# Filter matrices from sixteen skewed copies of the taps, and v kept unflipped in the first phase

## The reference, cut to what matters

```
q_in = silu(causal_dwconv(h @ Wq, wq_conv))     # 4 taps; k_in and v_in alike
q, k = l2norm(q), l2norm(k)
inv  = -(k*beta @ k.T) * strict_lower           # per chunk of 32 tokens
for i in range(1, 32): inv[i] += inv[i] @ inv   # row by row
local_long  = causal_dwconv(v_in, fir_long)     # 64 taps, a filter of its own per channel
local_short = causal_dwconv(v_in, fir_short)    # 5 taps
```

## Time and profile before

| what | value |
|---|---|
| median of 3 runs | 1322.98 us (1320.78 to 1327.27) |
| the profiled execution's own time | 1323.56 us |
| its span, first to last instruction | 1321.8 us |
| busy, share of the span | PE 85%, DVE 72%, ACT 68%, POOL 49% |
| mean granted TensorE clock | 0.895 |
| first phase, second phase | 0 to 240.7 us, 240.7 to 319.8 us |

### The profile page before, as it was taken

The page is one execution under the profiler, slowest core; times in us unless marked ns, Lnnn a source line. Parts: engine busy times, 40 slices in busy tenths (PEclk is TensorE's granted clock), DMA queues, the critical chain, the costliest instruction groups (busy, mean ns, idle before and its releaser), DMA issues. The chain is left out here.

```text
span 1321.8 us, 28637 instructions
## 1 busy us (share of the span) xinstructions
PE 1119.9 (85%) x9251; PEld 820.2 (62%) x9251; DVE 958.0 (72%) x2132; ACT 898.0 (68%) x1743; POOL 653.0 (49%) x2200
## 2 busy tenths in 40 slices
PE   5998988783678799999999999999999888885756
PEld 4776766683566566766776776676677655443225
DVE  5999998698355657777877877777787566633985
ACT  5999998221344558787878878877887665453867
POOL 4777775563225544465465466547546543111007
PEclk9999998555557869999999999999999988897989
DMA  2443433893412434343433434343442342203106
GB/s 80 159 176 144 177 136 144 185 234 107 137 57 85 110 80 127 95 124 109 133 110 106 146 105 138 106 129 105 111 144 82 96 127 57 65 33 140 44 1 223
DMA packets 141779, 154.17 MB, mean 117 GB/s; under 512 B 48040, under 2 KB 106560, under 8 KB 141632
## 3 DMA queue, kind: packets, MB, share of 16 engines
q1 hardware_dynamic: 141632, 152.35, 38.4%
HBM read 93.32 MB, written 58.72 MB: 115 GB/s over the span
## 5 line engine op out<-in xcount | busy, mean ns | idle before, releaser
L2120 DVE TENSOR_REDUCE x_maxima<-x_psA 128x2 f32<-128x512 f32 x248 | 170.3, 687 | 96.2 <-PE x_psA L1448 93.7
L1704 ACT ACTIVATE x_PT<-x_psB 128x512 f32<-128x512 f32 x240 | 143.0, 596 | 56.5 <-PE x_psB L1472 52.1
L1711 ACT ACTIVATE x_psA<-x_mask_q 128x512 f32<-128x512 bf16 x239 | 142.4, 596 | 51.8 <-DVE x_maxima L2120 48.7
L297 DVE SCALAR_TENSOR_TENSOR a_conv<-a_ps_proj,taps,a_conv 128x253 f32<-128x253 f32 (+2 forms) x288 | 115.0, 471 | 8.4 <-ACT a_conv L364 8.4
L1448 PE MATMUL x_psA<-x_Ks,x_Qs 96*128 96x256 bf16 x496 | 99.5, 283 | 15.2 <-ACT x_psA L1711 14.7
L1469 PE MATMUL x_psB<-x_mask_k,x_ident_bf 128*128 128x512 bf16 x240 | 94.3, 393 | 13.0 <-ACT x_PT L1704 10.8
L533 PE MATMUL a_ps_proj<-a_hT,wqkv 128*128 128x256 f32 x384 | 93.2, 392 | 7.1 <-DVE a_conv L297 4.2
L1472 PE MATMUL x_psB<-x_Qs,x_Ks 98*128 98x256 bf16 x480 | 94.1, 277 | 0.0
L533 PEld LDWEIGHTS a_ps_proj<-a_hT,wqkv 128*128 128x128 f32 x384 | 71.5, 194 | 19.4 <-issue 6.6
L1864 POOL TENSOR_SCALAR x_parts_q<-x_rest 128x512 bf16<-128x512 f32 x16 | 23.9, 1494 | 116.3 <-DVE x_rest L2096 116.3
L1486 PE MATMUL x_psO<-x_PT,x_V 128*32 128x256 f32 x1024 | 72.0, 401 | 1.0 <-ACT x_PT L1704 1.0
(11 more groups left out here) (390 smaller groups left out, 3352.8 us busy)
## 6 DMA issues: line engine op xcount, KB each, us to landing
scratch_keypack<-a_keypack SPq DMA_DIRECT2D x16, 768.0 KB, 3.3
c_keypack<-scratch_keypack SPq DMA_DIRECT2D x16, 768.0 KB, 4.7
x_Ks<-scratch_k_parts SPq DMA_DIRECT2D x192, 64.0 KB, 2.2
b_matrix<-in_long_padded SPq DMA_DIRECT2D x16, 512.0 KB, 7.4
scratch_k_parts<-x_parts_k SPq DMA_DIRECT2D x32, 192.0 KB, 2.4
scratch_q_parts<-x_parts_q SPq DMA_DIRECT2D x32, 192.0 KB, 2.3
x_Qs<-scratch_q_parts SPq DMA_DIRECT2D x32, 192.0 KB, 3.0
a_x_in<-in_x SPq DMA_DIRECT2D x16, 256.0 KB, 2.7
```

Source lines behind the costliest of these rows:

```text
L297: nc.vector.scalar_tensor_tensor(acc, ps_proj[PROJ_BANK[p]][:, c, 0:L - j], taps[:, p, c, TAPS - 1 - j:TAPS - j], acc, ALU.mult, ALU.add). ...
L1704: nc.scalar.activation(PT[:, k % (2 * GROUP)], bank_B(b, k)[0], ACT.Exp, scale=XD ** -0.5).then_inc(pexp_ready, 1)
L1711: nc.scalar.activation(psA[:].rearrange("p t q -> p (t q)"), mask_q[:, k % 2].rearrange("p s k -> p (s k)"), ACT.Copy).then_inc(mask_writt ...
L2120: nc.vector.tensor_reduce(maxima[:, t, 2 * pair:2 * pair + 2], bank_A(b, k)[0], AX.X, ALU.max).then_inc(maxed, 1)
```

## The change

The filter matrices get their reversal from memory instead of from PE. The taps are copied once, DRAM to DRAM, into 16 copies one behind the other for each channel. A transfer to 16 neighbouring partitions then reads with a step of `FIR_COLS - 1` from one copy to the next, which is one tap back per partition, the direction that unflipped v needs. The matrices of all 256 channels stay in SBUF (`keep["matrix"]`, 64 KB per partition) and are loaded in the first phase, one transfer per turn (`taps`, stage 1: 16 partitions by 128 channels by 64 taps). All flips and their evictions go; `vtok` writes straight into `v_windows`, `st_v` stores from there, and two small DMAs (`win`) make the second, shifted window. The second phase has no matrix loads: groups of 8 channels in each of two halves, one matmul of 64 columns per channel, eight PSUM banks. To make room, `diag` and all but one quarter of `M` live in `X32`, so the transposes of DVE (first and last) wait for one another, and POOL waits for all four; other small buffers share space.

```diff
-           ... (2, "turn_h"), (2, "hTc"), (5, "flipA"), (4, "ktok"), (5, "st_p"), (4, "st_k"),
+           ... (2, "turn_h"), (2, "hTc"), (4, "ktok"), (5, "st_p"), (4, "st_k"), (1, "taps"),
-           (4, "stok"), (1, "xn"), (4, "flipB"), (2, "gbias"), (4, "ks"), (4, "ksT"), (3, "tok1"), (4, "fB"), (3, "sq1"),
+           (4, "stok"), (1, "xn"), (2, "gbias"), (4, "ks"), (4, "ksT"), (3, "tok1"), (3, "sq1"),
...
+                elif op == "taps":
+                    row, half = b // FC, b % FC
+                    sp.wait_ge(taps_copied, 16)
+                    taps_of = bass.AP(dram["taps_copies"].tensor, half * P * COPIES * FIR_COLS + P - 1 - COPIES * row,
+                                      [[FIR_COLS - 1, COPIES], [COPIES * FIR_COLS, P], [1, HB]])
+                    sp.dma_start(keep["matrix"][COPIES * row:COPIES * row + COPIES, half * P:half * P + P], taps_of).then_inc(taps_placed, 16)
+                elif op == "win":
+                    sp.wait_ge(v_tok_ready, b + 1)
+                    sp.dma_start(keep["v_windows"][HB:P, 0, :, b], keep["v_windows"][0:HB, 1, :, b]).then_inc(window_set, 16)
+                    sp.dma_start(keep["v_windows"][0:HB, 0, 1, b], keep["v_windows"][HB:P, 1, 0, b]).then_inc(window_set, 16)
...
-            sp.dma_start(flip[:], dram["flip"]).then_inc(w_loaded, 16)
-            sp.dma_start(half_flip[:], dram["half_flip"]).then_inc(w_loaded, 16)
+            sp.dma_start(dram["taps_copies"], bass.AP(dram["long_padded"].tensor, 0, [[FIR_COLS, D], [0, COPIES], [1, FIR_COLS]])).then_inc(taps_copied, 16)
...
-                    nc.scalar.activation(v_tok[:], ps_tok[2][:], ACT.Copy).then_inc(v_tok_ready, 1)
-                elif op == "fA":
...
+                    nc.scalar.activation(keep["v_windows"][:, 1, :, b], ps_tok[2][:], ACT.Copy).then_inc(v_tok_ready, 1)
...
-CG = 16
-GROUPS = D // CG
-DEPTH = 4
+CG = 8
+GROUPS = P // CG
+DEPTH = 8
...
+            for stage in range(2):
+                sp.wait_ge(kept, (stage + 1) * (GROUPS // 2))
+                for half in range(FC):
+                    for part in range(2):
+                        at = slice(half * P + stage * HB, half * P + stage * HB + HB)
+                        sp.dma_start(dram["long_tok"][part * HB:part * HB + HB, :, :, at].rearrange("p t b c -> p (t b) c"),
...
+                for i in range(CG):
+                    for half in range(FC):
+                        c = half * P + group * CG + i
+                        last = nc.tensor.matmul(psum[n][half * HB:half * HB + HB, i], keep["matrix"][:, c],
+                                                keep["v_windows"][:, :, :, :, c].rearrange("p a t b -> p (a t b)"),
                                                 start=True, stop=True, skip_group_check=True)
...
-            nc.gpsimd.memset(lower[:], 0.0).then_inc(lower_set, 1)
             for s in used:
                 pool.sem_clear(s)
+            nc.gpsimd.memset(lower, 0.0).then_inc(lower_set, 1)
...
-            pool.wait_ge(M_turned, 1)
+            pool.wait_ge(M_turned, NQ)
...
-            for q in (NQ - 1, 0, 1, 2):
+            for q in range(NQ):
+                if q > 0:
+                    dve.wait_ge(M_turned, q)
...
+            for n, q in enumerate(reversed(range(NQ))):
                 at = slice(q * CH, (q + 1) * CH)
+                if n > 0:
+                    dve.wait_ge(X_turned, n)
```

More of the change, by code:

```diff
@@ L185, in phase_a @@
         SHORT_STEPS = FC * (SHORT - 2)
+        taps_copied = sem("taps_copied")
+        taps_placed = sem("taps_placed")
         DEEP = max(stage for stage, op in A_ORDER)
@@ L544, in part @@
                     else:
[L545 removed]
+                        after(b, (v_tok_ready, -1, 1))
                     for t in range(TT):
@@ new lines, in _ @@
+            sp.dma_start(early["k_tok"][:, 0], dram["k_tok"][0]).then_inc(early["pack_loaded"], 16)
+            sp.dma_start(early["hT0"][:], dram["hT"][0]).then_inc(early["hT_loaded"], 16)
+            sp.dma_start(keep["shared"][:, 0, 0], dram["v_tok"][0]).then_inc(early["vs_loaded"], 16)
+            sp.dma_start(keep["shared"][:, 0, 1], dram["short_tok"][0]).then_inc(early["vs_loaded"], 16)
+            for stage in range(2):
[4 more added lines that the diff above has]
+                        sp.dma_start(dram["long_tok"][part * HB:part * HB + HB, :, :, at].rearrange("p t b c -> p (t b) c"),
+                                     keep["long"][half * HB:half * HB + HB, part, :, stage * HB:stage * HB + HB]).then_inc(long_stored, 16)
@@ L679, in _ @@
                 n = group % DEPTH
-                pe.wait_ge(loaded[n], 16 * (group // DEPTH + 1))
                 if group >= DEPTH:
                     pe.wait_ge(kept, group - DEPTH + 1)
-                for c in range(CG):
-                    for part in range(2):
-                        last = nc.tensor.matmul(psum[n][part * HB:part * HB + HB, c].rearrange("p t b -> p (t b)"),
-                                                matrix[n][:, c], keep["v_windows"][:, part, :, :, group * CG + c].rearrange("p t b -> p (t b)"),
+                for i in range(CG):
[3 more added lines that the diff above has]
+                                                keep["v_windows"][:, :, :, :, c].rearrange("p a t b -> p (a t b)"),
                                                 start=True, stop=True, skip_group_check=True)
@@ L2460, in program @@
             keep["gates8"] = sb(mixer, "gates8", [P, B, TT, 2 * H])
+            keep["X32"] = sb(mixer, "X32", [P, B * NH, CH], side="right")
             keep["rq"], keep["rkb"] = (sb(mixer, n, [P, B, NH]) for n in ("rq", "rkb"))
             with ExitStack() as filters:
-                flip = sb(filters, "flip", [P, P])
-                half_flip = sb(filters, "half_flip", [P, P])
                 keep["v_windows"] = sb(filters, "v_windows", [P, 2, TT, B, D])
-                keep["diag"] = sb(filters, "diag", [P, B * NH, CH])
+                keep["matrix"] = sb(filters, "matrix", [P, D, HB])
                 sems_a = Semaphores(nc, filters)
-                phase_a(nc, sems_a, dram, keep, ident, flip, half_flip, ident_loaded)
-                keep["X32"] = sb(mixer, "X32", [P, B * NH, CH], side="right")
+                phase_a(nc, sems_a, dram, keep, ident, ident_loaded)
                 early = {n: sb(mixer, "c_" + n, shape, side="right")
@@ L2476, in program @@
                     early[n] = sems_c.new("c_" + n)
-                keep["long"] = sb(filters, "long_all", [P, TT, B, D], side="right")
+                keep["long"] = sb(filters, "long_all", [P, 2, TT * B, P], side="right")
                 sems_b = Semaphores(nc, mixer)
```

135 lines of the change are left out of this document (46 added, 89 removed).

## The result

The changed kernel took 1341.91 us (median of 4 runs, 1341.32 to 1346.59), the kernel before 1324.16 (4 runs, 1320.78 to 1327.27): ratio 1.0142, 95% interval 1.0107 to 1.0177. It is slower by more than the 0.5% that the prediction's chances went by; forecast were 1334.4 us, 1324 to 1343, with 0.68 for slower. In a later session the same pair gave 1.0158 (1.0118 to 1.0198). The profiled executions took 1323.56 and 1342.11 us, 18.55 apart.

A forecast was written before the change was run, and what follows sets the result against it. POOL's own chain, 13.23 us per batch, was taken to bound the first phase's steady part, with DVE next. 1323.56 + 9.4 + 2.3 - 2.4 + 1.5 = 1334.4 us; own range 1329 to 1340, 8 in 10 runs 1324 to 1343.

The forecast's parts named there:

- Start, +11.7 forecast: First phase's start: x of batch 2 waits behind copy and `taps`, +9.4 us; PE's lower clock adds +2.3.
- x behind `taps`: First phase's start: `taps` lands in 4.3 us, x about 1 us later plus 0.2 for issue, at 25.7.
- rival D: First phase's start: `taps` slow at 7.4 us, x 3.1 us later, total 1337.5 us; chance 0.08.
- some 3 us: First phase's start: by the skill page's 5.0 us for 512 KiB to 16 partitions, the sum would be this much higher.
- PE's lower clock, forecast at +2.3: First phase's start: after idling, PE's second projection ends 1.8 to 2.8 us late, lengthening DVE's wait; range 0 to 4.
- the period stays at 13.23: First phase's steady part: removed flips and evictions are not on POOL's list, so they are worth 0 us.
- near 0.7: First phase's steady part: DMA share with `taps` and `win` added, up from 0.44, costing 0 us.
- Rival E: Steady part: PE idle before `ksT` drops its clock; beyond 2.6 us slack, 1 us per batch, 1345 us; chance 0.08.
- End, -2.4 forecast: First phase's end: half flip (0.85 us), flip before `diag` (0.95) and last eviction (0.6) gone; range -3.5 to 0.
- Second phase, +1.5 forecast: Second phase: transposes waiting for each other, one more memset, and POOL beside DVE (0.6 us); range 0.5 to 2.5.
- with nothing to wait for: Second phase: PE's filters end by 296 us, stores land by about 307, under DVE's 319.5; worth 0 us.
- rival C: Third phase: wider filter matmuls lift the clock so it begins at 2.4 GHz, 23 us less, 1311 us; chance 0.07.

The follow-up runs named there:

- wide_after_copy: Changed kernel with each 512 KB matrix load going to all 128 partitions instead of 16; `taps` issue to first gate bias 6.0 us instead of 9.4, steady part 189.9 us.
- before_tail: Kernel before with the product of v and the short filter's last tap moved from POOL to ACT; ratio 0.9973 to the kernel before.
- one_load: Changed kernel without the copy and with one 128-partition matrix load, 15 of 16 loads left out; ratio 1.0082 to the kernel before.
- pe_fill: Changed kernel with two unread 512-column matmuls per batch on PE where the flips stood; ratio 1.0131 to the kernel before.
- short2_first: Changed kernel with DVE's last short-filter addition swapped ahead of the LayerNorm statistics; ratio 1.0148 to the kernel before.
- pe_waits: Changed kernel with PE starting the second phase's filters only after DVE's four first transposes; second phase 80.0 us against 82.5, timed once only.
- before_waits: Kernel before plus the unread copy, SP's wait for it, and second-phase waits of first transposes and POOL; ratio 1.0068 to the kernel before.

## Why the prediction was right, and where its sum was off

The sign and the largest term were forecast for the right reason. That 1341.91 lies inside 1324 to 1343 is luck in part: it is past the likeliest side (1329 to 1340), and a loss of 7.4 us that the sum had at nothing was offset by 5.1 us less in a stretch that the change doesn't touch. Without these 5.1 the profiled execution would have been at 1347. In the later session the medians lay 21.7 us apart, against 10.8 forecast.

**Start, +11.7 forecast, +14.5 measured.** Mechanism right. The copy landed by 20.98 (forecast 20.2, from 11.5 us and 1 us for the loads ahead; together they measured 13.1). The mis-sized term is x behind `taps`: 5.5 us from one landing to the other by the forecast, 8.4 measured, of which `wide_after_copy` puts 3.4 on the 16-partition form. That is rival D's mechanism at 0.08. By the Trainium skill, page "SBUF — State Buffer", section "Door 1: The DMA port swizzle (why `[64,N]` ≈ `[32,N]`)", 5.0 us was the estimate for such a transfer; the 16 measured landed in 7.2 to 12.0, and one to 128 partitions in 4.9. The trace agrees with the page's direction. It does not contradict its rate: with the prediction's 2 us fixed, 7.2 leaves 5.2. The "some 3 us" that the prediction adds by the page has no working; 5.0 in place of its 4.3 would be 0.7, and only the fixed 2 us on top make it 2.7. PE's lower clock, forecast at +2.3, cost 1.5 (14.53 at the second gate bias less 13.0 at the first).

**Steady part, 0 forecast, +7.4 in this profile (+1.1 to +7.4 over executions of the same first phase).** This is the step that failed: "the period stays at 13.23". The bound was rightly POOL's (`before_tail`). Traffic was rightly free (`one_load`, `wide_after_copy`, and `pe_fill` with the clock at 1.00), though the DMA share came to 0.92 to 0.98 and not "near 0.7". But a list that waits for nobody was taken for a list of fixed length. POOL's small operations stretch when DVE's two-input steps lie over them, so its length depends on DVE's place beside it, and that place changed with PE's list and its clock. Rival E had named PE's idle time ahead of `ksT` and the clock, at 0.08, and let it decide only beyond 2.6 us of slack through a wait; `pe_fill` shows that PE's filled list brings back the clock, DVE's place and POOL's length together. Of the 7.4 us 6.0 are POOL's longer instructions (420 of them, 158.8 to 164.8 us). That the overlap with DVE is what stretches them is shown for single ones (`short2_first`, the 2.34 us step); that it is the clock and not PE's later place in the turn that moves DVE is argued from the waits (1.3 us a turn for ACT behind a projection of 2.9 us, 0.7 behind one of 1.9), since the fill changes both.

**End, -2.4 forecast:** -2.1. **Second phase, +1.5 forecast, +3.8 measured:** with PE held back 1.3 are left for the waits (`pe_waits`); `before_waits` also gave 1.3, with the last transposes still without theirs. The 2.5 on top are the filters beside the transposes (`pe_waits`), which the prediction had at nothing: of PE, "with nothing to wait for", it took only the end. In the kernel before, PE waited for its matrices until 245 us, and only the fourth transpose was longer (2.24 us); now it filters beside all four. The filters' time fits neither branch of the forecast, 55 us or 27: it was 37.6, off the path. **Rest, 0 forecast:** nothing attributable. The clock of the second phase was 1.00 during the filters, but 0.50 again ahead of the third (305 to 343 us), and rival C did not come.

The sum by measured terms, 14.5 + 7.4 - 2.1 + 3.8 = 23.6, less 5.1 in a stretch that varies by 12, is the 18.5 seen. The landmarks cut one span into pieces, so that they add up is no proof; the causes rest on the experiments.

## What to carry to other kernels

A wait in an in-order DMA queue and the data queued behind it are two costs: moving the wait away gave back less than half, since the x load then lay behind 3 MB of copy. An engine without waits is not an engine of fixed length; look at the spread of one instruction's time across turns before calling a period safe. And work taken off an engine that idles anyway can cost: here the turns were regular and the clock at 1.00 only with the work, or a filler, in its place; compare stage by stage where the whole varies by more than the effect.

## What the runs showed of the hardware

- A copy of 3.1 MB from DRAM to DRAM, in 768-byte runs, landed 13.1 us after its issue, loads ahead included (13.1 to 14.2 in nine profiled executions); in 12 to 20 us the queues moved 320 to 361 GB/s. 512 KB to 16 partitions in flight with x made a DMA share of 1.42 at only 97 GB/s.
- POOL's products of 128x16 took 0.2 us beside DVE's other steps. Beside DVE's steps with two SBUF inputs they took more: 0.5 to 0.7 (the copy of 128x8 too) under the single addition of 0.7 us, and under the row of six short filter steps 0.2 to 0.45 in most turns but 2.55 and 2.34 in two (60.52 and 156.59 us). The Trainium skill, page "SBUF — State Buffer", section "🔬 SBUF: two separate sides", describes an exclusive lock held for an instruction. The 0.5 to 0.7 us agree. The 2.34 us agree only if the lock is passed on within DVE's row of six, which no run tests, and why most turns show so much less stays open.
- PE's matmuls slowed DVE's SBUF-to-SBUF transposes of 128x1024 from 1.90 us to 2.40 to 2.83. The same section of the Trainium skill names only the pair of DVE and GpSimd as engines that contend; here the measurement decides. In the kernel before, 32-column matmuls ran beside the third transpose from 245.02 on and beside all of the fourth; the third took 1.87 us, the fourth 2.24 (2.19 in `before_waits`, where POOL was still); that PE is the cause there too is not shown. The lower clock does not spare the transposes: at 0.50 the first transpose of the changed kernel took 2.44. Why the third was spared stays open.
- After an idle time of PE of 2.42 us the granted clock was 1.00, after one of 2.51 us a turn later 0.50, and after 1.08 us in the changed kernel's usual turns 0.53 as well. The matmuls of 64 columns in the second phase began at 0.50 (260.6 to 262.9 us) and ran at 1.00, that is 2.4 GHz, from 265 on; those of 32 columns before ran at 0.50 throughout.
